# Normalization passes on GpSimd, smaller FFN weight rings, output stage fused: a transformer block on eight cores

## What is computed

```python
xn = _layernorm(x, axis=-1)
q = rope(xn @ Wq.T);  k = rope(xn @ Wk.T);  v = xn @ Wv.T
o1 = softmax(q1 @ k1.T * scale) @ v;   o2 = softmax(q2 @ k2.T * scale) @ v
attn = rmsnorm(o1 - lam * o2) * gamma * (1 - LAMBDA_INIT)
ffn  = ((silu((xn @ gate_w.T) * gate_s)) * ((xn @ up_w.T) * up_s)) @ down_w.T * down_s
x = x + attn @ Wo.T + ffn
```

## Time and profile before

| | us |
|---|---|
| runs of the kernel before | 6365.96 and 6416.35, median 6391.15 |
| the profiled execution | 6300.0 |
| its span, core 5 (the slowest) | 6298.3 |
| spans of the eight cores | 6270.5 to 6298.3 |

### The profile page before, as it was taken

One profiled execution on the slowest core, in us unless ns is written; L12 is line 12 of the kernel. 1 busy time (PEld: TensorE's weight loads), 2 busy tenths in 40 slices (PEclk: granted clock), 3 DMA queues, 4 the chain that ended last, 5 costly groups with the idle time before them and its releaser, 6 DMA issues.

```text
span 6298.3 us, 47919 instructions; the slowest of 8 cores (6270.5 to 6298.3 us)
## 1 busy us (share of the span) xinstructions
PE 4217.8 (67%) x16260; PEld 1349.7 (21%) x16260; DVE 1077.5 (17%) x1876; ACT 1734.2 (28%) x1863; POOL 206.6 (3%) x402
## 2 busy tenths in 40 slices
PE   2557356545745575567797778878787787878782
PEld 0113112211311131123342333211111111111121
DVE  3330432233133303311101110000000000000011
ACT  1101111211121111100000000456666666666620
POOL 0000000000000000010011000000000000000000
PEclk6769678867867697789999999888888888888886
DMA  4245212411331131155575557210000100000024
GB/s 134 67 107 167 95 40 85 148 61 42 127 125 39 60 114 27 20 101 97 97 137 103 98 100 130 48 27 14 14 14 14 27 14 14 14 22 19 1 38 122
DMA packets 177301, 428.87 MB, mean 68 GB/s; under 512 B 75944, under 2 KB 75944, under 8 KB 170152
## 3 DMA queue, kind: packets, MB, share of 16 engines
q0 software_dynamic: 55872, 272.65, 20.2%
q1 hardware_dynamic: 121192, 153.16, 8.2%
HBM read 539.02 MB, written 58.72 MB: 95 GB/s over the span
## 4 chain that ended last, share of the span: by engine, by line
PE 65%; DVE 14%; ACT 10%; issue 5%; DMA 5%; DVEq 1%; ACTq 0%; SPq 0%; POOLq 0%; POOL 0%
PE ps_a L1050 9%; PE ps_a L1446 7%; PE ps_b L1277 6%; PE ps_a L1141 6%; PE ps_a L1146 5%; PE ps_a L1251 5%; PE ps_d L1287 5%; PE ps_b L1282 4%; PE ps_d L1291 4%; PE ps_b L1185 2%; PE ps_a L288 2%; PE ps_b L1192 2%; DMA xc<-xTb 2%; PE ps_a L1365 2%; ACT e L1271 2%
## 5 line engine op out<-in xcount | busy, mean ns | idle before, releaser
L1271 ACT ACTIVATE e<-ps_a,bias_sb 128x1024 bf16<-128x1024 f32 x1024 | 1141.0, 1114 | 457.6 <-PE ps_a L1256 452.1
L1141 PE MATMUL ps_a<-xn_bf,wffn 128*128 128x512 bf16 x1408 | 567.9, 403 | 282.1 <-DVE h_bf L1167 258.5
L252 PE MATMUL ps_d<-sq_b,mask_bf 128*1 128x512 bf16 x160 | 93.6, 585 | 707.7 <-ACT sq_b L247 523.9
L1146 PE MATMUL ps_a<-xn_bf,wffn 128*128 128x512 bf16 x1408 | 566.8, 403 | 0.0
L1251 PE MATMUL ps_a<-q_bf,ktb 64*128 64x512 bf16 x1024 | 415.1, 412 | 111.8 <-DVE xn_bf L1336 98.7
L1050 PE MATMUL ps_a<-xnb,wbuf 128*128 128x512 bf16 x1536 | 435.5, 454 | 77.5 <-DVE xnb L221 77.5
L1277 PE MATMUL ps_b<-e,vtb 128*128 128x512 bf16 x1024 | 403.6, 394 | 63.9 <-ACT e L1271 50.3
L1256 PE MATMUL ps_a<-q_bf,ktb 64*128 64x512 bf16 x1024 | 416.1, 413 | 0.0
L231 ACT ACTIVATE qraw_bf<-ps_a 128x1024 bf16<-128x1024 f32 x80 | 81.9, 1024 | 1210.7 <-PE ps_a L1050 981.7
L1282 PE MATMUL ps_b<-e,vtb 128*128 128x512 bf16 x1024 | 404.6, 395 | 0.0
L1291 PE MATMUL ps_d<-e,ones_col_bf 128*1 128x512 bf16 x1024 | 402.3, 393 | 0.0
(11 more groups left out here) (121 smaller groups left out, 3782.9 us busy)
## 6 DMA issues: line engine op xcount, KB each, us to landing
wffn<-gu POOLq DMA_DIRECT2D x176, 512.0 KB, 7.0
xc<-xTb SPq DMA_DIRECT2D x64, 1024.0 KB, 5.6
wvbuf<-wv_c POOLq DMA_DIRECT2D x28, 2048.0 KB, 8.8
wffn<-dn POOLq DMA_DIRECT2D x64, 704.0 KB, 9.5
wbuf<-wk_c POOLq DMA_DIRECT2D x48, 512.0 KB, 3.6
kT_s<-kstage SPq DMA_DIRECT2D x64, 256.0 KB, 2.3
v_s<-v_stage SPq DMA_DIRECT2D x32, 512.0 KB, 6.9
ktb<-kT_s SPq DMA_DIRECT2D x16, 1024.0 KB, 5.2
```

Of the source, the lines that this page charges most:

```text
L1141: p.emit("pe", lambda E, kch=kch, par=par, tile=tile, gsl=gsl: E.matmul(t["ps_a"][:, par * 1024: par * 1024 + 512], wffn[:, gsl * 2048 + k ...
L1146: mm = lambda E, kch=kch, par=par, tile=tile, usl=usl: E.matmul(t["ps_a"][:, par * 1024 + 512: par * 1024 + 1024], wffn[:, UOFF + usl * 20 ...
L1271: ev = p.inc("act", "ac", 1, lambda E, par=par, h=h: E.activation(t["e12"][:, par * 1024:(par + 1) * 1024], ps_a[:, par * 1024:(par + 1) * ...
```

## The change

- **Normalization.** The casts of pass 1 and both operations of pass 2 move from VectorE to GpSimd. GpSimd does not read PSUM here: ScalarE copies the two spread rows to two new tiles, `mB_sb` and `rB_sb`, and a new tile `plt` takes the difference. What follows waits for `pl` and not for `dv`.
- **Head maxima.** In `emit_headnorm` TensorE's wait for VectorE names the last value that a head maximum left (`hn_dv`), not the newest. The same wait is put ahead of each tile of the normalization.
- **FFN rings.** The gate ring goes from 3 to 2 blocks, the down ring from 4 to 3 halves; `wffn` shrinks from 11264 to 8448 columns.
- **Output.** The last loop goes into the Wo loop: per block, SyncE loads `x`, VectorE adds `acc` and PSUM into `out_sb`, then `x`, and SyncE stores. The Wo matmuls two blocks on wait for the second add.

The same edits in two functions that this mode does not run are left out of the listing, as are repeated tile declarations.

```diff
--- before.py
+++ after.py
@@ -172,18 +175,19 @@
     for tile in range(2):
+        p.wait("pe", "dv", t.get("hn_dv", 0))
         for q in range(4):
             i, sl, key = qload(q, tile)
-            p.wait("dve", *key)
+            p.wait("pool", *key)
             p.wait("act", *key)
             for j in range(4):
                 kch = q * 4 + j
                 co = sl * 2048 + j * 512
-                p.inc("dve", "dv", 1, lambda E, co=co: E.tensor_copy(
+                p.inc("pool", "pl", 1, lambda E, co=co: E.tensor_copy(
                     xbb[:, co:co + 512], xc[:, co:co + 512]))
                 p.inc("act", "ac", 1, lambda E, co=co: E.activation(
                     x2b[:, co:co + 512], xc[:, co:co + 512], AF.Square))
-                p.wait("pe", "dv")
+                p.wait("pe", "pl")
                 p.wait("pe", "ac")
                 p.emit("pe", lambda E, co=co, kch=kch: E.matmul(
                     ps_d1[:], t["ones_col_bf"][:], xbb[:, co:co + 512],
@@ -191,7 +195,7 @@
                 mmv = p.inc("pe", "pe", 1, lambda E, co=co, kch=kch: E.matmul(
                     ps_d2[:], t["ones_col_bf"][:], x2b[:, co:co + 512],
                     start=(kch == 0), stop=(kch == KCH - 1)))
-            ring.consumed(i, "dv", "ac", "pe")
+            ring.consumed(i, "pl", "ac", "pe")
...
@@ -204,25 +208,29 @@
         p.inc("act", "ac", 1, lambda E: E.activation(row[0:1, 1536:2048], row[0:1, 1536:2048], AF.Exp, scale=-0.5))
         p.wait("pe", "ac")
         p.wait("pe", "dv")
+        p.wait("pe", "pl")
         p.emit("pe", lambda E: E.matmul(ps_b[:, 0:512], t["ones_row_f"][:], row[0:1, 0:512],
                                         start=True, stop=True))
         bcv = p.inc("pe", "pe", 1, lambda E: E.matmul(
             ps_b[:, 512:1024], t["ones_row_f"][:], row[0:1, 1536:2048], start=True, stop=True))
+        p.wait("act", "pe", bcv)
+        p.inc("act", "ac", 1, lambda E: E.activation(t["mB_sb"][:], ps_b[:, 0:512], AF.Copy))
+        brv2 = p.inc("act", "ac", 1, lambda E: E.activation(t["rB_sb"][:], ps_b[:, 512:1024], AF.Copy))
         for q in range(4):
             i, sl, key = qload(q, tile)
-            p.wait("dve", *key)
-            p.wait("dve", "pe", bcv)
+            p.wait("pool", *key)
+            p.wait("pool", "ac", brv2)
             for j in range(4):
                 kch = q * 4 + j
                 co = sl * 2048 + j * 512
                 c0 = xn_col0 + tile * 512
-                p.inc("dve", "dv", 1, lambda E, co=co: E.tensor_tensor(
-                    t["tmp0"][:, 0:512], xc[:, co:co + 512], ps_b[:, 0:512], ALU.subtract))
-                p.inc("dve", "dv", 1, lambda E, kch=kch, c0=c0: E.tensor_tensor(
+                p.inc("pool", "pl", 1, lambda E, co=co: E.tensor_tensor(
+                    t["plt"][:, 0:512], xc[:, co:co + 512], t["mB_sb"][:], ALU.subtract))
+                p.inc("pool", "pl", 1, lambda E, kch=kch, c0=c0: E.tensor_tensor(
                     xn_bf[:, kch * xn_seg + c0: kch * xn_seg + c0 + 512],
-                    t["tmp0"][:, 0:512], ps_b[:, 512:1024], ALU.mult))
-            ring.consumed(i, "dv")
-    return {"dv": p.ct["dv"]}
+                    t["plt"][:, 0:512], t["rB_sb"][:], ALU.mult))
+            ring.consumed(i, "pl")
+    return {"pl": p.ct["pl"]}
...
@@ -264,6 +272,7 @@
         p.inc("dve", "dv", 1, lambda E, col=col: E.tensor_tensor(
             t["srow"][0:1, col:col + 1], t["srow"][0:1, col:col + 1],
             t["trow"][0:1, 2:3], ALU.max))
+        t["hn_dv"] = p.ct["dv"]
     return p.ct["pe"]
...
@@ -930,6 +942,9 @@
     t["srow"] = ent(nc.sbuf_tensor("srow", [1, 64], F32))
     t["trow"] = ent(nc.sbuf_tensor("trow", [1, 16], F32))
     t["eps_col"] = ent(nc.sbuf_tensor("eps_col", [128, 1], F32))
+    t["mB_sb"] = ent(nc.sbuf_tensor("mB_sb", [128, 512], F32))
+    t["rB_sb"] = ent(nc.sbuf_tensor("rB_sb", [128, 512], F32))
+    t["plt"] = ent(nc.sbuf_tensor("plt", [128, 512], F32))
...
@@ -1117,12 +1132,12 @@
     scope_barrier(p)
     t["acc"] = ent(nc.sbuf_tensor("acc", [128, 16 * 1024], F32))
     t["h_bf"] = ent2(nc.sbuf_tensor("h_bf", [128, ICH * 512], BF16, side="right"))
-    t["wffn"] = ent2(nc.sbuf_tensor("wffn", [128, 11264], BF16, side="right"))
-    gring = Ring(p, "rg", 3, "pool")
+    t["wffn"] = ent2(nc.sbuf_tensor("wffn", [128, 8448], BF16, side="right"))
+    gring = Ring(p, "rg", 2, "pool")
     uring = Ring(p, "ru", 2, "pool")
-    dring = Ring(p, "rd", 4, "pool")
+    dring = Ring(p, "rd", 3, "pool")
     wffn = t["wffn"]
-    UOFF = 6144
+    UOFF = 4096
...
@@ -1351,12 +1366,20 @@
     ent4 = ctx4.enter_context
     scope_barrier(p)
     t["wbuf2"] = ent4(nc.sbuf_tensor("wbuf2", [128, 4096], BF16, side="right"))
+    t["xe"] = ent4(nc.sbuf_tensor("xe", [128, 2048], F32, side="right"))
+    t["out_sb"] = ent4(nc.sbuf_tensor("out_sb", [128, 2048], F32, side="right"))
     wring = Ring(p, "rw", 2, "pool")
     wofree = [{"ac": ac_free, "dv": dv_free}, {"ac": ac_free, "dv": dv_free}]
+    stv = []
     for och in range(16):
         par = och % 2
         wi, wsl, wkey = wring.load(lambda s: (lambda E, och=och, s=s: E.dma_start(
             out=t["wbuf2"][:, s * 2048:(s + 1) * 2048], in_=wo[och])))
+        if och >= 2:
+            p.wait("sync", f"st{par}", stv[och - 2])
+        xv = p.inc("sync", f"ldx{par}", 16, lambda E, och=och, par=par: E.dma_start(
+            out=t["xe"][:, par * 1024:(par + 1) * 1024],
+            in_=xTb[och * 128:(och + 1) * 128, 0:1024]))
...
@@ -1373,37 +1396,23 @@
                     p.emit("pe", mm)
         wring.consumed(wi, "pe")
         p.wait("dve", "pe", ov)
-        fv = p.inc("dve", "dv", 1, lambda E, och=och, par=par: E.tensor_tensor(
-            t["acc"][:, och * 1024:(och + 1) * 1024],
+        p.wait("dve", f"ldx{par}", xv)
+        if och >= 2:
+            p.wait("dve", f"st{par}", stv[och - 2])
+        p.inc("dve", "dv", 1, lambda E, och=och, par=par: E.tensor_tensor(
+            t["out_sb"][:, par * 1024:(par + 1) * 1024],
             t["acc"][:, och * 1024:(och + 1) * 1024],
             ps_a[:, par * 1024:(par + 1) * 1024], ALU.add))
-        wofree[par] = {"dv": fv}
-    ctx4.close()
-
-    ctx5 = ExitStack()
-    ent5 = ctx5.enter_context
-    scope_barrier(p)
-    t["xe"] = ent5(nc.sbuf_tensor("xe", [128, 2048], F32, side="right"))
-    t["out_sb"] = ent5(nc.sbuf_tensor("out_sb", [128, 2048], F32, side="right"))
-    stv = []
-    for och in range(16):
-        par = och % 2
-        if och >= 2:
-            p.wait("sync", f"st{par}", stv[och - 2])
-        v = p.inc("sync", f"ldx{par}", 16, lambda E, och=och, par=par: E.dma_start(
-            out=t["xe"][:, par * 1024:(par + 1) * 1024],
-            in_=xTb[och * 128:(och + 1) * 128, 0:1024]))
-        p.wait("dve", f"ldx{par}", v)
-        p.wait("dve", "dv", wofree[par].get("dv", 0))
-        ev = p.inc("dve", "dv", 1, lambda E, och=och, par=par: E.tensor_tensor(
+        fv = p.inc("dve", "dv", 1, lambda E, och=och, par=par: E.tensor_tensor(
             t["out_sb"][:, par * 1024:(par + 1) * 1024],
-            t["acc"][:, och * 1024:(och + 1) * 1024],
+            t["out_sb"][:, par * 1024:(par + 1) * 1024],
             t["xe"][:, par * 1024:(par + 1) * 1024], ALU.add))
-        p.wait("sync", "dv", ev)
+        p.wait("sync", "dv", fv)
         stv.append(p.inc("sync", f"st{par}", 16, lambda E, och=och, par=par: E.dma_start(
             out=outT[och * 128:(och + 1) * 128, :],
             in_=t["out_sb"][:, par * 1024:(par + 1) * 1024])))
-    ctx5.close()
+        wofree[par] = {"dv": fv}
+    ctx4.close()
```

## The result

| | us |
|---|---|
| kernel before, median of 10 runs | 6429.3 |
| changed kernel, median of 11 runs | 6558.3 |
| ratio, with its 95% interval | 1.037 (1.031 to 1.043) |
| spans of the two profiled executions, slowest core | 6298.3 and 6543.0 (+244.7, 3.9%) |

The change made the kernel slower by 3.7%. The forecast was 6587 us and +3.1%, and its range of 6460 to 6680 holds the 6558. The sum of the forecast is made for the span: +196 us, against the +245 measured. So its sign held, its percentage lies at the lower edge of the interval, and its sum was a fifth too small. The next table says where.

A forecast was written before the change was run, and what follows sets the result against it. No engine was taken to bound the whole span, though TensorE held 65% of the chain of waits. Terms 155 + 19 + 96 - 74 = +196 us, on the 6391 us median, gave 6587 us (+3.1%), range 6460 to 6680.

The forecast's parts named there:

- Normalization: Pass 2 and casts on GpSimd, plus ScalarE's copies: 155 us over eight tiles; pass 2 at 1.32 us per instruction, 17 per tile.
- The casts of pass 1: Normalization, casts moved to GpSimd: partly hidden by x loads and ScalarE's squares, 1.0 us per tile (0 to 3).
- The copies by ScalarE: Normalization, ahead of pass 2: two copies of broadcast rows from PSUM plus one handover, 1.4 us per tile.
- The K loads: K projection: each chunk's first weight load is issued only after GpSimd's last multiply, so TensorE waits its landing; 19 us.
- Rival (a): Normalization: GpSimd keeps nearly VectorE's pace, 1 us instead of 17 per tile; sum +66, 6457 us; chance 0.15.
- Down projection: Ring of 4 to 3: the second half's load comes late, 2.8 us per stall, 30 stalls, 84 us; 96 with slower matmuls.
- rival (b): Down projection: queue as full as before, late half lands at 10.7 us, stalls 201 us; sum +313, 6704 us; chance 0.2.
- (c): Down projection: the late half's load is hidden anyway, so no stall; sum +100, 6491 us; chance 0.05.
- The failed term: Down projection: slower matmuls when TensorE returns from a stall, 0.4 us per stall (0 to 0.6), 12 us together.
- Wo and output: Output loop folded into the Wo stage: period 9.6 us (8.6 to 11.5), a gain of 74 us (46 to 89).
- contention: Fused Wo and output loop: Wo's loads delay the x load by 1.0 us per period (0 to 2.9).
- Rival (d): Fused output loop at 7.3 us with TensorE as bound: 35 us more gain, sum +161, 6552 us; no chance of its own.

## Why the forecast came out as it did

**The total, nearer than it earned.** The 6587 us is 29 above the 6558, but two errors stand against each other in it. The sum was 49 us too small. And it was put on top of a median 91 us above the profiled execution; the changed kernel's median is only 14 us above its own (6544.5), so the base was 77 too high. That the microseconds came so close is luck; the +196 against +245 is what to judge by.

**Normalization, right in mechanism; its size came out by errors that offset.** Predicted +155 and +19, measured +184 up to the FFN. Of this, 175 us lie in the four stretches from the start, or the last V matmul of a chunk, to the next K matmul (together 511 us before and 686 after, medians of the eight cores). Pass 2 of a tile went from 25.2 us (642.08 to 667.31) to 44.9 (756.03 to 800.90), 157 us in eight tiles where 136 were taken: its step is 1.41 us (1.263 busy and 0.14 of gap) where 1.32 was taken. Other terms came out smaller. The casts of pass 1 were charged with 8 us and cost nothing visible: at 0.616 us they stay under ScalarE's 0.630 of the earlier trace rows. The copies by ScalarE took the 1.5 us that they were priced at (679.30 to 680.80), but the stretch between the passes grew by 0.8 us only, 6 us and not 11. The K loads cost 18 us of the 19. The other 9 us of the 184 lie mostly in the V projections, 140 to 143 us each against 137; the forecast had nothing for them, and why they grew the runs don't show. Rival (a), GpSimd at VectorE's pace, is out.

**Down projection, the stall right, what follows it not.** The wait was predicted at 2.8 us and 84 in all; the profile shows 81.7 us in 30 waits. The landing of the late half is 6.1/6.4/9.1 us, so taking 6.8 instead of the median 7.8 of the earlier trace rows was right, rival (b) falls, and with 30 waits so does (c). The failed term is the next one: 12 us for the matmuls behind the stalls. The FFN grew by 128, so they cost 128 - 82 = 46 us, 1.5 per stall: the 22 matmuls behind a wait take 6.2 us and not 4.75. The term was read off the gate and up stage of the earlier trace rows by subtraction, 0.6 us or so per block, of which 0.4 was taken. That is a mean over blocks that are not alike, which the trace of the kernel before shows. Two neighbouring blocks of its core 5: the timeline with the first two matmuls of each, then the table of stages for each block's 32 matmuls.

```profile
2908.95 0.59 PE L1141 MATMUL ps_a<-xn_bf,wffn 128*128 128x512 bf16 x1 [2.98 <-DVE h_bf L1167]
2909.33 0.63 PE L1146 MATMUL ps_a<-xn_bf,wffn 128*128 128x512 bf16 x1
...
2920.55 0.38 PE L1141 MATMUL ps_a<-xn_bf,wffn 128*128 128x512 bf16 x1 [2.98 <-DVE h_bf L1167]
2920.77 0.38 PE L1146 MATMUL ps_a<-xn_bf,wffn 128*128 128x512 bf16 x1
```

```profile
2908.95:2917.58 8.63, 8.62 (x32) 3.41 (x32) 0.00 (x0) 0.00 (x0) 0.00 (x0) 0.82 0.56 111
2920.55:2927.62 7.07, 7.07 (x32) 3.03 (x32) 0.00 (x0) 0.00 (x0) 0.00 (x0) 1.00 0.68 136
```

Both blocks follow a wait of 2.98 us. The first runs at a mean granted clock of 0.82 and loses 1.6 us, the second at 1.00 and loses nothing. In this tile 14 of 43 waits are followed by slow matmuls, which lose 1.3 to 3.0 us, 30 us together; the other 29 cost nothing behind them. In the down stage of the changed kernel all 15 waits of the first tile on core 4 are followed by slow matmuls, for 1.4 to 2.3 us each, and 12 of 15 on core 0. So where a wait costs something behind it, it costs no less in the gate and up stage; what the forecast missed is how many of the waits do. Why so few in one stage and nearly all in the other the runs don't show.

**Wo and output, right.** Predicted -74, measured -71. The period was to be 9.6 us with 1.0 of it for contention. It is 9.7 to 10.4 on the eight cores, 9.9 in the median, so by the 8.6 of the forecast contention was 1.3. The run without Wo's loads gives it directly: a period of 8.4, so 1.5. The slowest core had 172 us. Rival (d), a period of 7.3 with TensorE as the bound, is out; it took the load ahead of the store to get there.

**What was costed at nothing.** The head norms' new wait and the gate ring did cost nothing: the gate and up part of the two tiles took 467 and 471 us on core 4, against 472 and 465 on core 5 of the kernel before.

**The signs that were named.** GpSimd busy about 400 us in the normalization: 402. A normalization of 162 us: 161.5 from the last matmul of the chunk before to the last multiply (639.4 to 800.9), 166.3 with the wait for the K load. A down period of 12.7 us and a stage of 204: 13.7 and 222, the missed term. Gate and up at 473: 467. No tail, and VectorE waiting for x: so it is, with 118.6 us of waits for `xe` on core 4.

## What to carry to other kernels

Price a new wait of TensorE twice: for its length, and for the matmuls behind it. For the second price look at single blocks: the mean over another stage, most of whose waits cost nothing behind them, gave 0.6 us a block, and a wait cost 1.5 here. When a ring loses a slot, follow which consumer frees which load; here the point of release mattered and the number of slots did not. A slower engine may pay as a helper on a quarter of the work where it loses as a replacement. And a chain through one queue (load behind store) was worth more reordered here (109 us) than hidden beside the matmuls (72 us).

## What the runs showed of the hardware that was not expected

In the down stage most waits of TensorE of 2.1 to 3.5 us are followed by some eight matmuls 0.43 us apart instead of 0.216 (the lower of the two clock levels), for 1.4 to 1.9 us of lost time. After a wait of almost 7 us the loss is 1.7 or 2.8 us by turns, with 6.54 and 7.68 us for 22 matmuls. In a tile of the gate and up stage 29 of 43 waits of 3 us are followed by no slow matmul at all. GpSimd's gap between dependent instructions of 1.26 us is 0.14 us. GpSimd and VectorE, the latter with one input in PSUM, ran side by side with no loss on either (0.687 and 1.265 us). The GpSimd queue's loads reach 151 GB/s through three slots of 704 KB, and with stores and x loads beside them the last stage of the run with the x load ahead reached 191.
